# A transformer megakernel on one core: the order of the shared expert's low parts and the one-hots ahead of the routed experts, and the warming products there

## What is computed

```python
STAGES = ['ffn:L0','attn0','ffn:L0','moe:L1','attn1','ffn:AFT','moe:L1','moe:L2','attn2','moe:L2','moe:L3','attn3','moe:L3']
```

```python
logits = xf @ gate_w.T
probs = jax.nn.softmax(logits.astype(jnp.float32), axis=-1)
topk_p, topk_i = jax.lax.top_k(probs, K)
...
h = jax.nn.silu(h1) * h2
eo = jnp.einsum('eni,eci->enc', h, w3)
y = jnp.einsum('enc,ne->nc', eo, comb).reshape(Bq, Tq, Cq)
sh = jax.nn.silu(xf @ sw1.T) * (xf @ sw2.T) @ sw3.T
return y + sh.reshape(Bq, Tq, Cq)
```

## Time and profile before

| | |
|---|---|
| median of 3 runs | 3240.19 us (3236.42 to 3241.41) |
| the profiled execution | 3237.12 us, of it the span 3235.3 us |
| TensorE busy | 2859.1 us, 88% of the span |
| VectorE busy | 2223.7 us, 69% |
| ScalarE, GpSimd busy | 1503.0 us (46%), 1531.7 us (47%) |
| mean granted TensorE clock | 0.924 |

### The profile page before, as it was taken

The page is one execution under the profiler, slowest core; times in us unless marked ns, Lnnn a source line. Parts: engine busy times, 40 slices in busy tenths (PEclk is TensorE's granted clock), DMA queues, the critical chain, the costliest instruction groups (busy, mean ns, idle before and its releaser), DMA issues.

```text
span 3235.3 us, 60360 instructions
## 1 busy us (share of the span) xinstructions
PE 2859.1 (88%) x20922; PEld 2556.8 (79%) x20922; DVE 2223.7 (69%) x6068; ACT 1503.0 (46%) x3245; POOL 1531.7 (47%) x1493
## 2 busy tenths in 40 slices
PE   8979999999999899896698987769997858976898
PEld 6869999999999888795487876757776847966697
DVE  6767777777777767665735667568886765664665
ACT  3355666656666533344523434445454534443342
POOL 2345565655555405635600445658884545350134
PEclk9989999999999899897798987979998978989899
DMA  4022222222212210363004343810002553650533
GB/s 152 1 70 73 56 58 65 56 73 56 73 52 70 89 41 5 102 212 130 20 0 152 115 125 109 251 37 2 2 2 72 185 139 83 194 193 0 215 95 105
DMA packets 147766, 285.81 MB, mean 88 GB/s; under 512 B 20673, under 2 KB 70209, under 8 KB 144385
## 3 DMA queue, kind: packets, MB, share of 16 engines
q1 hardware_dynamic: 113458, 211.38, 19.8%
q0 software_dynamic: 21216, 57.96, 6.8%
q10 hardware_dynamic: 12816, 12.78, 1.2%
HBM read 191.59 MB, written 90.45 MB: 87 GB/s over the span
## 4 chain that ended last, share of the span: by engine, by line
PE 67%; DVE 17%; ACT 5%; DMA 4%; issue 3%; POOL 3%; SPq 0%; DVEq 0%; ACTq 0%; POOLq 0%
PE bank L552 17%; PE bank L553 17%; PE bank L554 17%; PE bank L2555 3%; PE bank L2571 2%; PE bank L1292 2%; DMA MXG<-dxn,IDX 2%; PE bank L1005 1%; DMA YG<-dyo,POSI 1%; POOL YG L1750 1%; PE bank L692 1%; PE bank L1314 1%; PE bank L723 1%; DVE ST L603 1%; PE bank L1211 1%
## 5 line engine op out<-in xcount | busy, mean ns | idle before, releaser
L1738 POOL DMA_INDIRECT MXG<-dxn,IDX x250 | 237.4, 949 | 248.7 <-PE bank L1292 211.8
L1750 POOL DMA_INDIRECT YG<-dyo,POSI x192 | 187.2, 975 | 177.1 <-DMA dyo<-YS 106.3
L2702 POOL TENSOR_SCALAR SX<-SX,MN 128x256 f32<-128x256 f32 x256 | 233.8, 930 | 46.1 <-DVE MN L2633 46.0
L1581 POOL TENSOR_TENSOR SHL<-SGS,SHH 128x512 fp32r<-128x512 f32 x18 | 25.0, 1391 | 391.1 <-ACT SHH L1386 391.1
L2633 DVE CUSTOM_DVE_ANT_0 SX<-bank,FMASK 128x128 f32<-128x128 f32 (+1 forms) x512 | 156.2, 351 | 48.0 <-PE bank L2546 47.9
L1104 POOL TENSOR_TENSOR HL<-HID,HH 128x512 fp32r<-128x512 f32 x56 | 72.4, 1292 | 240.3 <-ACT HH L1069 240.1
L552 PE MATMUL bank<-MWH,GH 128*128 x500 | 170.7, 341 | 0.7 <-DVE HB L1655 0.6
L1422 ACT ACTIVATE GH<-bank 128x256 fp32r<-128x256 f32 x250 | 95.6, 384 | 141.2 <-PE bank L1292 140.5
L552 PE MATMUL bank<-MWH,SHH 128*128 128x256 f32 x352 | 108.8, 309 | 53.8 <-DVE SHL L1581 27.6
L554 PE MATMUL bank<-MWH,GL 128*128 x500 | 154.8, 310 | 0.0
L553 PE MATMUL bank<-MWL,GH 128*128 x500 | 154.7, 309 | 0.0
(11 more groups left out here) (464 smaller groups left out, 11586.1 us busy)
## 6 DMA issues: line engine op xcount, KB each, us to landing
dyo<-YS SPq DMA_DIRECT2D x250, 128.0 KB
RAW<-in_wheads SPq DMA_DIRECT2D x68, 320.0 KB, 6.1
BB<-dgates SPq DMA_DIRECT2D x68, 256.0 KB, 3.6
GB<-dgates SPq DMA_DIRECT2D x68, 256.0 KB, 4.4
RAW<-in_eL SPq DMA_DIRECT2D x32, 304.0 KB, 2.9
dkeptL<-MWL SPq DMA_DIRECT2D x32, 304.0 KB
dkeptL<-MWH SPq DMA_DIRECT2D x32, 304.0 KB
MWH<-dkeptL SPq DMA_DIRECT2D x8, 1216.0 KB, 12.7
```

Of the source, the lines that this page charges most:

```text
L1738: nc.gpsimd.indirect_dma_start(MXG[:, n % XGS, :], None, dxn, bass.IndirectOffsetOnAxis(ap=IDX[:, b:b + 1], axis=0)).then_inc(x_in[n % XGS ...
L1750: nc.gpsimd.indirect_dma_start(YG[:, i % YGS, :], None, dyo[0:m.blocks * P, :], bass.IndirectOffsetOnAxis(ap=POSI[:, c * NT + t:c * NT + t ...
L2702: nc.gpsimd.tensor_scalar(part, part, MN[:, n % RING2, 1:2], None, ALU.subtract).then_inc(s_less1, 1)
```

## The change

Three edits, all in the openings.

1. `low_by_pool` is gone: VectorE runs every `shared_low`. It stands between the two halves of a one-hot chunk: `moe_hot` is split in `moe_block_hot` (HOT, AHOT) and `moe_slot_hot` (BHOT), one chunk in each of the steps 0 to 3. In L2 the low part of step 0 is moved ahead of `moe_slots`.
2. `moe_inverse` 0 and 1 stand in step 3 (gated) or step 4 (L2), 2 and 3 in step 5: ahead of `shared_down(4)` when gated, behind it in L2. `moe_index` is still in step 4 on VectorE when gated, and in L2 it is moved from step 5 to step 4.
3. `warm(24, 1)` is gone when gated and is `warm(8, 1)` in L2.

```diff
-        INVERSE_AT = {True: (3, 4), False: (3, 5)}
-
-        def low_by_pool(st, s):
-
-            return s < LOWS_BY_VECTOR + 2 and (st.cached or s >= LOWS_BY_VECTOR)
+        INVERSE_AT = {True: 3, False: 4}
...
                 shared_up(pe, st, s, moe_prefix if s == 0 else None)
-                if s in INVERSE_AT[m.gated]:
-                    n = 2 * INVERSE_AT[m.gated].index(s)
-                    moe_inverse(pe, st, n)
-                    moe_inverse(pe, st, n + 1)
+                if s == INVERSE_AT[m.gated]:
+                    moe_inverse(pe, st, 0)
+                    moe_inverse(pe, st, 1)
+                if s == 5 and m.gated:
+                    moe_inverse(pe, st, 2)
+                    moe_inverse(pe, st, 3)
                 if s:
                     shared_down(pe, st, s - 1)
+                if s == 5 and not m.gated:
+                    moe_inverse(pe, st, 2)
+                    moe_inverse(pe, st, 3)
             shared_down(pe, st, m.early - 1)
-            warm(24, 1)
+            if not m.gated:
+                warm(8, 1)
...
+            if not m.gated:
+                shared_low(dve, st, 0)
             moe_slots(dve, st)
             for s in range(m.early):
+                c = s if s < 4 else None
                 shared_product(dve, st, s)
-                if not low_by_pool(st, s):
-                    shared_low(dve, nc.vector, st, s)
                 if s == 0 and st.name == 'L3':
                     nc.vector.tensor_scalar(SGT[:, :], SGT[:, :], 0.5, None, ALU.mult)
-                if s < 2:
-                    moe_hot(dve, st, s)
-                if s == 2:
-                    if m.J == 2:
-                        shared_add(dve, st, 0)
-                    moe_hot(dve, st, 2)
-                    moe_hot(dve, st, 3)
-                if s == 3 and m.J == 3:
-                    shared_add(dve, st, 0)
-                if s == (4 if m.gated else 5):
+                if c is not None:
+                    moe_block_hot(dve, st, c)
+                if s == 4 and not m.gated:
                     moe_index(dve, st)
+                if s + (not m.gated) < m.early:
+                    shared_low(dve, st, s + (not m.gated))
+                if s == 4:
+                    if m.gated:
+                        moe_index(dve, st)
                     moe_experts(dve, st)
-                if s > 3 and s % m.J == 0:
+                if m.J == 3 and s == 3 or m.J == 2 and s in (1, 3):
+                    shared_add(dve, st, (s + 1) // m.J - 1)
+                if c is not None:
+                    moe_slot_hot(dve, st, c)
+                if m.J > 3 and s and s % m.J == 0:
                     shared_add(dve, st, s // m.J - 1)
...
             for s in range(m.early):
-                if low_by_pool(st, s):
-                    shared_low(pool, nc.gpsimd, st, s)
```

More of the change, by code:

```diff
@@ L157 @@
 LAGS, DEEP = 2, 3
-LOWS_BY_VECTOR = 2
 GROUP = W // P
@@ L1536, in moe_slots, with moe_block_hot @@
             step(nc.vector.scalar_tensor_tensor(LOF[:, :], PBI[:, :], -float(P), POS[:, :], ALU.mult, ALU.add))
-        def moe_hot(dve, st, c):
-            chunks = 2 * NT // CHUNK
+        def moe_block_hot(dve, st, c):
             if c >= 2:
-                dve.wait_ge(r_hot_read, chunks * st.moe + c - 1)
+                dve.wait_ge(r_hot_read, 2 * NT // CHUNK * st.moe + c - 1)
             cols = slice(c * CHUNK, (c + 1) * CHUNK)
@@ L1548, in moe_hot, with moe_slot_hot @@
                                          IDF[:, tiles].unsqueeze(2).to_broadcast([P, CHUNK, NBP]), ALU.mult))
+        def moe_slot_hot(dve, st, c):
+            cols = slice(c * CHUNK, (c + 1) * CHUNK)
             nc.vector.tensor_tensor(BHOT[:, c % 2, :, :], LOF[:, cols].unsqueeze(2).to_broadcast([P, CHUNK, P]),
@@ L1573, in shared_product, with shared_low @@
                 nc.vector.tensor_tensor(SGS[:, a, :], SGS[:, a, :], bank[2 + a][:, :], ALU.mult).then_inc(h_done, 1)
-        def shared_low(queue, engine, st, s):
+        def shared_low(dve, st, s):
             a = s % 2
[L1578 to L1581, removed]
+            dve.wait_ge(hh_done, st.steps + s + 1)
+            nc.vector.tensor_tensor(SHL[:, a, :], SGS[:, a, :], f32(SHH[:, a, :]), ALU.subtract).then_inc(h_ready, 1)
         def shared_add(dve, st, w):
@@ L1694, in moe_vector @@
                 if k < m.late:
-                    shared_low(dve, nc.vector, st, m.early + k)
+                    shared_low(dve, st, m.early + k)
                 for w in range(m.pre, NW):
```

## The result

The changed kernel takes 3244.76 us at the median of 20 runs (3233.66 to 3252.52), the kernel before, measured beside it, 3237.28 (3232.32 to 3244.38). The ratio is 1.0021 [1.0013, 1.0028]: the change costs some 7 us (6.8 by the ratio, 7.5 between the medians). That it is slower is clear of the noise; whether it is over 0.2% is not, since the interval has that value inside. The profiled execution took 3240.86 us, 3.7 more than that of before.

A forecast was written before the change was run, and what follows sets the result against it. It took TensorE (67% of the chain) and VectorE (17%) to bound the kernel. Opening terms of -6.8 us and +3.5 for the clock gave -3.3, on the median 3240.19 a forecast of 3237 us, range 3229 to 3245.

The forecast's parts named there:

- +1.4 us a stage: Gated stages: a new wait of shared_down(2) for its low part, queued behind HOT and AHOT of chunk 2; +1.4 us.
- My relief: L2a: GpSimd, last there, loses two low parts, so the gather could start 3.5 us earlier; term -1.0 us.
- The rule of the Trainium skill that I set against this: L2a: two-input VectorE instructions and GpSimd instructions reading SBUF exclude each other; it would put L2a at +3 us.
- the term that I put at nothing: L2b: 8 warming products instead of 24 give nothing, since VectorE comes last.
- -1.6 for a clock: L1a: its window behind the old gap ran at 0.50; -1.6 us more, between nothing and the 1.8 of L3b.
- the chain as written: L2b: VectorE is the bound and its chain lengthens; IDX 3.4 us later, opening +2.7 us.
- The clock term: Four gated stages: TensorE at half clock behind new gaps without warming products; +3.5 us, bounds 0 and 7.
- The second rival: VectorE bounds both L2 stages, low parts and one-hots queuing behind weight low parts; +0.7 us, 3241, chance 0.10.
- the third: Rival: the clock falls behind most new gaps of the openings; +9.4 us, 3250, chance 0.12.

The follow-up runs named there:

- the runs with the filling: Kernel before and changed order in L2a alone, GpSimd there filling weight low parts with zeros instead of computing them; ratios to the kernel before 0.9970 and 0.9969.

## Why the prediction was wrong

**By the timed halves, both sums failed.** My terms give the gated half -8.5 and +3.5 for the clock, -5.0 us or -0.15%; it measured +0.02% [-0.07, +0.11]. They give L2 -1.0 + 2.7 = +1.7 us or +0.05%; it measured +0.37% [0.22, 0.52], some 12 us. L2 is the larger miss, and it has two parts: L2a's opening, and the products behind L2b. In the gated half the low part ahead of HOT in step 2 was worth some 5 us and the products behind the openings some 5 more (1.0002, 0.9985, 0.9970), each with intervals that overlap; my terms for both, +1.4 us a stage and +3.5 us in all, were too small if these are right.

**L2a, the step that failed.** I wrote "Bounds -4 and +3; I take -1.0, nearer to the middle than either". It measured +4.4, past the upper bound. My relief rested on GpSimd being last: IDX at 1990.42 and the gather at 1994.96. GpSimd did get lighter, and the gather now follows IDX by 3.0 us (1997.80 behind 1994.79) instead of 4.5. But IDX itself came 3.9 later against the stage's start. I had the stretched durations before me (HOT 1.63, AHOT 2.08, low part 1.77), costed them in L3a, and left them out of L2a's chain; nor did I ask what else the low part of step 0, moved ahead of `moe_slots` as a relief, would push into GpSimd's subtractions. The rule of the Trainium skill that I set against this pointed the right way, and its +3 was nearer than my -1.0; by the runs with the filling up to 3 us are this collision and 1 the chain.

**L2b, the term that I put at nothing.** "Eight products instead of 24 give nothing here, since VectorE comes last" looked at the first GL alone. There it holds (24 cost 0.5 us more). Behind it, in L2b alone, the missing 16 left the first blocks at 1.2 GHz, and the time is some 5 us longer in two pairs of runs. For the changed kernel itself this is not shown: with 24 it stayed at 1.0025.

**L1a, mis-sized.** Forecast -1.3, measured +0.6. I counted -1.6 for a clock that would no longer fall once the stall of 2.23 us was gone. The stall went, but the new wait of 1.77 took its place and the window behind it ran at 0.50 as well. A gap replaced by a gap four fifths as long gave no clock back. My sum for the gated stages counts a clock returned and, apart from that, a clock lost at the end of the opening; it has no term for one lost in step 2.

**Near in one profile.** In L3b and L3a -3.6 and -2.4 for -3.9 and -2.7; L1b -0.8 for -0.6; L2b +3.0 for +2.7, by the chain as written (IDX 3.7 later, forecast 3.4). L2b came out at +3.0 in every profile with 8 products, and is right. L3b is right step by step (2.8 us earlier at the last down step, 2.9 forecast), but against a profile in which the clock had fallen in its old order, which it often does not (last section). That L3a and L1b came so near is partly luck: L3a had only -0.6 with L3 alone (in the changed kernel its wait in step 2 is 3.35 us, nearly double that of the other gated stages), and L1b untouched varies by more than its term. The wait in step 2 is 1.77 where I had 1.4: the four tenths that I let TensorE fill with chunk 1 are not there. The warming products were worth VectorE's idle time and not their own 2.5 us.

**The clock term, right in kind, near in sum by luck.** +3.5 forecast for the new gaps, +2.5 measured outside the openings in the profile, and half-clock windows at the first blocks of L1a, L1b, L3a and L2b. I had looked for them only in the gated stages. But of the 2.5, 1.5 stand behind L2b and 0.5 ahead of the first opening, and the same rest of the kernel is 6.6 us shorter in the profile with L2a's order alone, which can touch there only what stands behind L2a (1.7 of the 6.6). A number of this size can't be read from one profile.

**The result as a sum.** With L2a and L1a as measured my sum is -6.8 + 5.4 + 1.9 = +0.5 in the openings, and with +3.5 for the clock +4.0; the two profiles differ by 3.7. The timed runs differ by 7, a median against a median, which one profile of each does not show in full. The two halves of the change add up to 0.02 + 0.37 = 0.39% where the whole has 0.21 [0.13, 0.28]; the second interval alone is 0.15 wide to either side. The base was off too: I started from 3240.19, the median of three runs, and twenty gave 3237.28. That 3244.76 lies just under my upper bound of 3245 is luck of this base: as a difference my bound was +5, and +7 was measured. The second rival, with VectorE the bound in L2, names what happened in L2a, but its +0.7 is far below +7. By the number the third is nearer, +9.4 for a clock that falls behind most new gaps; that it fell at so many places was not counted.

## What to carry to other kernels

An operation that is moved from GpSimd to VectorE must be costed at its duration beside GpSimd's reads, and so must everything queued with it; where a bound is worked out for one stage, use the same stretched rows in the next. An operation moved ahead as a relief also pushes back what stands behind it, here three operations of the routing into GpSimd's reads. Products that nobody reads can be worth more than they take, since the blocks behind an idle TensorE can run at half the clock (L2b alone, 0.50 and 5 us): price the stretch behind a gap before the gap itself is counted as a gain. And when two engines pass work in turns, try the order in which the awaited small operation stands ahead of the one that itself waits: here that swap, the 24 products and leaving the L2 stages alone turned +0.2% into -0.3% together.

## What the runs showed of the hardware

**The same gap in the same code may or may not halve the clock.** L3b is untouched in the kernel with L2a's order alone, and its gap is the same 2.23 us; the window behind it ran at 1.00, where it was 0.64 before, and the first GL came 3.0 us earlier against the stage's start. Half of these 3.0 were there ahead of that gap: the wait of step 0, 3.1 to 3.2 us in both, left the clock at 0.65 in a stretch of 4 us behind it before (3035.8 to 3039.8) and at 1.00 here. Nine of the kernels tried leave L3b and its products untouched; in five of their profiles it is some 3.0 us shorter than in the profile of before, in four as long.

```profile
3046.26 0.39 PE L552 MATMUL bank<-MWH,SHH 128*128 128x256 f32 x1 [2.23 <-POOL SHL L1597]
```

```profile
3047.70:3050.60 2.90, 2.90 (x16) 2.41 (x15) 1.26 (x4) 0.00 (x0) 1.93 (x2) 1.00 0.16 48
```

L1b, untouched in four others, came 1.4 to 3.0 us later. So one profile gives an opening's own length only to within some 3 us. L3's -3.6 in one profile is not proof of 3.6; only the timed runs (0.9985 with L3 alone) are.

**GpSimd's subtractions of weights cost far more than their place on the path.** Without their reading, and in 0.52 instead of 1.26 us each, L2a alone gives back 9.9 us in the old order (9.4 of them already at IDX) and 13.3 in the changed one, though TensorE waited for these low parts only 5 us in the whole kernel before (2.3 for products, 2.7 for weight loads). That is as much as the best order tried here gave, and no version was found that has it and computes the low parts.
